# First and third LayerNorm of a decoder layer applied by ScalarE in two passes, and all step tables written anew

## The reference

```
x = layernorm(x + attention(x))       # 16 heads, causal, top-32 keys of each row kept
x = layernorm(x + experts(x, gate))   # 8 experts: relu(x W1_e) W2_e, times gate
x = layernorm(x + ffn(x))             # Hadamard turn, 4-bit rows, ternary weights

def _layernorm(x, axis=-1, eps=1e-05):
    m = jnp.mean(x, axis=axis, keepdims=True)
    v = jnp.var(x, axis=axis, keepdims=True)
    return (x - m) / jnp.sqrt(v + eps)
```

## Time and profile before

| what | value |
|---|---|
| runs of the kernel | 601.8, 604.54 and 602.76 us, median 602.76 |
| profiled execution | 602.27 us, its span from first to last instruction 600.5 us |
| PE busy | 528.7 us (88% of the span) |
| DVE busy | 460.9 us (77%) |
| ACT busy | 388.8 us (65%) |
| POOL busy | 344.8 us (57%) |
| mean granted clock of PE | 0.945 |
| DMA moved | 21.84 MB, mean 36 GB/s |

### The profile page before, as it was taken

The page is one execution under the profiler, slowest core; times in us unless marked ns, Lnnn a source line. Parts: engine busy times, 40 slices in busy tenths (PEclk is TensorE's granted clock), DMA queues, the critical chain, the costliest instruction groups (busy, mean ns, idle before and its releaser), DMA issues. The chain is left out here.

```text
span 600.5 us, 22290 instructions
## 1 busy us (share of the span) xinstructions
PE 528.7 (88%) x8180; PEld 451.2 (75%) x8180; DVE 460.9 (77%) x2867; ACT 388.8 (65%) x941; POOL 344.8 (57%) x336
## 2 busy tenths in 40 slices
PE   5577459999999989999999989998999999989941
PEld 3455337888778878887888878887888888878830
DVE  1777986868988997698889888989899998623213
ACT  2788765866667667675677657776686777555620
POOL 3458661975566646556375646665656556656831
PEclk9699757999999999999999999999999999999975
DMA  8253440010000010000100100010001000000000
GB/s 234 69 196 116 133 132 18 24 38 20 3 20 20 3 55 21 2 3 3 55 20 3 56 3 21 3 55 3 19 3 39 2 4 2 20 1 2 19 0 17
DMA packets 21932, 21.84 MB, mean 36 GB/s; under 512 B 1856, under 2 KB 19776, under 8 KB 21824
## 3 DMA queue, kind: packets, MB, share of 16 engines
q1 hardware_dynamic: 21824, 20.42, 10.9%
HBM read 18.32 MB, written 2.10 MB: 34 GB/s over the span
## 5 line engine op out<-in xcount | busy, mean ns | idle before, releaser
L484 POOL TENSOR_TENSOR h_lo<-h_raw,h_hi 128x512 f16<-128x512 f32 x128 | 149.1, 1167 | 126.5 <-ACT h_raw L607 125.4
L801 PE MATMUL ps_o<-w_hi,h_lo 128*128 128x256 f16 x512 | 139.8, 273 | 4.7 <-POOL h_lo L484 4.5
L785 PE MATMUL ps_z<-x1t_hi,w_lo 128*128 128x256 f16 x512 | 140.4, 274 | 0.7 <-DVE x1t_lo L951 0.7
L785 PE MATMUL ps_z<-x1t_lo,w_hi 128*128 128x256 f16 x512 | 140.1, 274 | 0.0
L785 PE MATMUL ps_z<-x1t_hi,w_hi 128*128 128x256 f16 x512 | 140.1, 274 | 0.0
L801 PE MATMUL ps_o<-w_lo,h_hi 128*128 128x256 f16 x512 | 139.6, 273 | 0.0
L801 PE MATMUL ps_o<-w_hi,h_hi 128*128 128x256 f16 x512 | 139.6, 273 | 0.0
L603 ACT ACTIVATE h_hi<-ps_z 128x512 f16<-128x512 f32 x128 | 76.0, 594 | 69.1 <-PE ps_z L785 69.1
L893 DVE MATCH_REPLACE8 taken<-next,taken 128x64 f32<-128x64 f32 (+4 forms) x480 | 110.5, 242 | 0.1
L505 POOL TENSOR_TENSOR acc<-go_sb,acc 128x512 f32<-128x512 f32 x56 | 71.4, 1274 | 58.2 <-ACT go_sb L617 57.4
L888 DVE MAX8 next<-taken 128x8 f32<-128x64 f32 (+4 forms) x480 | 85.3, 243 | 0.0
(11 more groups left out here) (118 smaller groups left out, 980.0 us busy)
## 6 DMA issues: line engine op xcount, KB each, us to landing
w_raw<-in_w1t SPq DMA_DIRECT2D x8, 512.0 KB, 4.3
w_raw<-in_w2t SPq DMA_DIRECT2D x8, 512.0 KB, 5.8
xt_sb<-in_xt SPq DMA_DIRECT2D x8, 256.0 KB, 3.4
x_sb<-in_x SPq DMA_DIRECT2D x8, 256.0 KB, 3.0
out<-out_sb SPq DMA_DIRECT2D x8, 256.0 KB, 2.2
xa_sb<-in_xt SPq DMA_DIRECT2D x7, 256.0 KB, 2.8
ctx_sb<-in_ctx_w SPq DMA_DIRECT2D x8, 128.0 KB, 3.0
itok_sb<-in_itok SPq DMA_DIRECT2D x8, 128.0 KB, 3.4
```

What stands on the lines that cost most here:

```text
L484: nc.gpsimd.tensor_tensor(h_lo[:, e % 2, 2 * z:2 * z + 2, :], h_raw[:, z, :, :], h_hi[:, e % 2, 2 * z:2 * z + 2, :], ALU.subtract)\
L785: last = pe.matmul(ps_z[z][:, d * UT:(d + 1) * UT], w[:, e, c, at:at + P], x[:, c, :], start=n == 0, stop=n == len(terms) - 1)
L801: last = pe.matmul(ps_o[e % 2][:, b * D:(b + 1) * D], h[:, e % 2, c, b * SEQ:(b + 1) * SEQ], w[:, e, c, :], start=n == 0, stop=n == len(te ...
```

## The change

The apply of the first LayerNorm in all units, and that of the third in units 0 to 6, moves from DVE to ACT. DVE did both sequences with one instruction each, (x - mean) x rstd. ACT does x + (-mean) for both sequences, waits for itself, and then multiplies by rstd in place. POOL makes -mean, one more small instruction between adding epsilon and the power. The second LayerNorm, and the third of the last unit, stay on DVE.

```diff
-    ("pe", "out_proj"), ("dve", "ln1_stats"), ("pool", "rstd1"), ("dve", "ln1_apply"), ("pe", "turn_x1"),
+    ("pe", "out_proj"), ("dve", "ln1_stats"), ("pool", "rstd1"), ("act", "ln1_apply"), ("pe", "turn_x1"),
...
-    ("pool", "rstd3"), ("dve", "ln3_apply"), ("sp", "store"),
+    ("pool", "rstd3"), ("act", "ln3_apply"), ("sp", "store"),
...
-                put(base + at[name], engine, name, v)
+                put(base + at[name], "dve" if name == "ln3_apply" and v == UNITS - 1 else engine, name, v)
...
+                    if i != 1:
+                        nc.gpsimd.tensor_scalar(minus_mean[:, i, :], meanvar[:, i, :, 0], -1.0, None, ALU.mult)\
+                            .then_inc(eps_added[i], 1)
-                    pool.wait_ge(eps_added[i], v + 1)
+                    pool.wait_ge(eps_added[i], (2 if i != 1 else 1) * (v + 1))
...
+            def layernorm_apply(i, dst, src, v, ready):
+                act.wait_ge(rstd_ready[i], v + 1)
+                for b in range(UB):
+                    last = act.activation(dst[:, b, :], src[:, b, :], ACT.Identity, bias=minus_mean[:, i, b:b + 1])
+                last.then_inc(centred[i], 1)
+                act.wait_ge(centred[i], v + 1)
+                for b in range(UB):
+                    last = act.activation(dst[:, b, :], dst[:, b, :], ACT.Copy, scale=rstd[:, i, b:b + 1])
+                last.then_inc(ready, 1)
```

All tables are new. Two lines of `STEADY` stand for them:

```diff
-    "rstd1": 38.75, "ln1_apply": 42, "turn_x1": 41.75, "x1t_high": 42, "x1t_low": 43, "gate_scale": 46.5,
+    "rstd1": 40.25, "ln1_apply": 39.5, "turn_x1": 42, "x1t_high": 41, "x1t_low": 44, "gate_scale": 48.75,
```

More of the change, by code:

```diff
@@ L106 @@
 STEADY = {
[L107 to L111, removed]
@@ L112 @@
-    "rstd1": 38.75, "ln1_apply": 42, "turn_x1": 41.75, "x1t_high": 42, "x1t_low": 43, "gate_scale": 46.5,
-    "experts": 44, "relu": 0, "h_low": 0, "gate_out": 0.5, "gated_add": 0.5, "ln2_stats": 77, "rstd2": 77.5,
[3 rows of a table removed]
+    "shift0": 0.75, "shift1": 0.25, "shift2": 0.5, "shift3": -1.25, "scores": -6.75, "copy_scores": -7, "exp": 4.75,
+    "select": 3, "pace": 0.875, "keep": 7.25, "turn_probs": 9.5, "copy_probs": 8.5, "turn_probs2": 10.75,
+    "copy_probs2": 10.25, "attend": 13, "normalise": 13.75, "load_xt": -13.25, "q": -11.75, "copy_q": -12.5,
@@ L117 @@
+    "spread_q": -11.75, "k": 44.75, "copy_k": -20.25, "v": 94.5, "copy_v": 94.75, "load_x": -4.5, "load_ctx": 23,
+    "x_plus_bo": 25.5, "gate_sums": 29.5, "turn_o": 36.75, "copy_ot": 35.75, "out_proj": 38.75, "ln1_stats": 39.5,
+    "rstd1": 40.25, "ln1_apply": 39.5, "turn_x1": 42, "x1t_high": 41, "x1t_low": 44, "gate_scale": 48.75,
+    "experts": 44, "relu": -0.5, "h_low": 0.5, "gate_out": -0.5, "gated_add": 1.5, "ln2_stats": 78.75, "rstd2": 78.5,
[3 rows of a table added]
 }
 FIRST = STEADY | {
-    "shift0": 2.5, "shift1": 1.25, "shift2": 0.5, "shift3": -0.25, "scores": -3, "copy_scores": -1.75, "select": 3,
@@ L120 @@
[L120 to L124, removed]
@@ L125 @@
-    "hadamard": 80.75, "copy_ot": 35.25, "spread_q": -14.5, "q": -16.5, "ffn_residual": 89.75, "copy_q": -9.75,
-    "load_ctx": 29.25, "ln3_stats": 97, "ffn": 88, "ln1_apply": 41.75,
+    "k": -7.75, "v": -2.5, "copy_v": -0.25, "exp": 6.5, "h_low": -2, "gate_sums": 25.75, "x1t_low": 43,
+    "ln1_apply": 40.75, "copy_probs": 9.25, "copy_ot": 36.75, "copy_probs2": 11.5, "out_proj": 40.25,
+    "normalise": 13.25, "load_x": 11.25, "select": 2, "shift3": -0.5, "x1t_high": 41.25, "turn_o": 38.75,
@@ new lines @@
+    "turn_o": 37, "load_xt": -21.75, "copy_probs2": 10.75, "shift2": 0, "out_proj": 38.5, "scores": -5.25,
+    "x_plus_bo": 9.25, "to_q4": 81.75, "copy_scores": -5.25, "normalise": 14.75, "copy_q4t": 88, "ffn_scale": 91.5,
+    "x1t_low": 44.25, "pace": 1.25, "ln3_stats": 105.25, "ln1_stats": 39.75, "x2t_high": 78.5, "load_x": -6.25,
+    "quantise": 82.75, "x2t_low": 82, "ln3_apply": 109.25, "gate_out": -1, "store": 132.25, "keep": 7,
+    "copy_k": -16.25, "v": 93, "k": 44.25, "turn_q4": 89.5, "ln1_apply": 40, "rstd3": 105.75, "ffn": 92,
@@ L136 @@
+    "gate_sums": 29, "x1t_high": 40.75,
 }
 LAST = STEADY | {
-    "shift2": 0, "normalise": 11.75, "x_plus_bo": 20.25, "gate_sums": 31.5, "experts": 43.75, "copy_probs": 8.75,
-    "turn_probs2": 9, "shift1": 0.25, "copy_k": -11, "ffn": 94.75, "out_proj": 38.5, "attend": 13.5, "to_q4": 87.25,
-    "rstd2": 76.75, "copy_scores": -6, "ffn_residual": 78.5, "exp": 5, "ffn_scale": 88, "turn_o": 37.25,
-    "turn_x2": 77.5, "copy_q4t": 89.25, "ln3_stats": 99.25, "copy_v": 32, "rstd1": 39.25, "store": 116.25,
@@ L142 @@
-    "ln1_apply": 41, "ln2_apply": 76.75, "quantise": 85.25, "ln2_stats": 71.5, "v": 11.75, "load_xt": -11.75,
-    "gate_scale": 49.75, "x2t_high": 82.5, "spread_q": -13.5, "rstd3": 98.75, "keep": 7.75, "copy_q": -12.25,
-    "ln1_stats": 37.5, "hadamard": 81.5, "k": 25, "x2t_low": 81.25, "gate_out": -0.5,
+    "shift1": 2.5, "exp": 2, "shift0": 3, "shift2": 1.5, "shift3": 1, "copy_q": -10.25, "turn_probs": 6.5,
+    "select": 0.5, "copy_probs": 5.25, "q": -8.75, "spread_q": -9, "copy_scores": -7.75, "scores": -8,
@@ L365, in decoder_layer @@
         rstd_ready = [sem(f"rstd_ready{i}") for i in range(3)]
+        centred = [sem(f"centred{i}") for i in range(3)]
         MISC = {
```

37 lines of the change are left out of this document (25 added, 12 removed), and 9 rows, old and new, of tables (SECOND, STEADY).

## The result

The changed kernel took 586.77 us in the median of 4 runs (585.7 to 590.07), the kernel before 602.85: a ratio of 0.973, with a 95% interval of 0.970 to 0.976. A second set of 6 runs (e1) gave 588.84 against 603.1, 0.976 (0.973 to 0.979). Medians and ratios are those of fast executions, and one slow execution of e16, of 2968 us, is left out.

A forecast was written before the change was run, and what follows sets the result against it. PE was taken as the bound from first expert matmul to last L2 (busy 464.17 of 477.5 us), after a chained head. Middle 6.4 plus head 4.1 gave 10.5: 602.3 - 10.5 = 591.8, range 588 to 595.5 (0.56).

The forecast's parts named there:

- (1): Sign on ACT: each apply runs as two pairs near 0.85 us each, with 0.03 between them.
- (2): Sign on PE: waits for x before turning x1 gone in units 1 to 7; about 0.3 us for h_lo instead.
- (3): Sign on PE: busy within 7 us of the length from the first L1 to the last L2.
- (4): Sign in the head: first L1 near 92 us, second mask on DVE near 39.6.
- (5): Sign at the end: the last unit's serial tail takes 27 to 28 us.
- The middle: First expert matmul to last L2: PE's waits at x1 turns shrink, 1.5 to 0.3 us in units 2 to 5; 6.4 gained.
- Rival D: More gain than forecast: the middle gives 10 of its 13.3 us and the head 6, 586.3; chance 0.10.
- The head: Chain through all engines before the first expert matmul: the new order gains 4.1 us, bounds -2 and 6.
- The walk's own 4.7: Head's new order laid along old durations to L1 of expert 3: 4.7 us gained, before allowing for low-clock steps.
- Third LayerNorm: hidden: Third apply on ACT, between an exp block and expert 1's relu: relu hidden with 1.8 us to spare.
- Rival C: Slower: ACT comes late to the apply behind an exp block; 0.7 us to spare in each unit; chance 0.08.
- The ScalarE rule: Skill's advice of VectorE for add and mul; without cover, seven hand-overs 1 us later each, 599.3.

The follow-up runs named there:

- e1: The changed kernel run again with no edit, for a second profile and more times: 588.84 us, ratio 0.976 to the kernel before.
- e16: The changed code with every engine's steps in the order of before, first and third applies on ScalarE: 617.12 us, ratio 1.023.
- e7: The changed kernel plus two unread tensor_scalar steps with constants on VectorE behind the first LayerNorm's sums: 587.13 us.
- e8: The changed kernel with VectorE waiting, without work, for GpSimd's 1/sigma behind the first LayerNorm's sums: 592.14 us.
- e11: The changed kernel plus four unread activations on ScalarE ahead of the first LayerNorm's apply: 595.02 us, ratio 0.986.
- e9: The changed kernel with the first apply back on VectorE, two steps later in its line in units 1 to 6: 590.89 us, ratio 0.981.
- e6: The changed kernel with only the third apply back on VectorE, in the same place of the order: 596.96 us, ratio 0.989.
- e3: The changed kernel's new order with both the first and third applies back on VectorE: 618.94 us, ratio 1.025 to the kernel before.
- e10: The changed kernel with both applies back on VectorE, each at a later place in its line: 594.37 us, ratio 0.984.
- e2: The changed kernel with only the first apply back on VectorE, ahead of the next unit's mask: 610.69 us, ratio 1.012.
- e18: The changed kernel with single-activation ScalarE applies and unread matmuls in the head's gaps on PE: 585.36 us, ratio 0.968.

## Why the prediction was right in direction and short in size

The mechanism was right; two terms of the sum were mis-sized. In units 2 to 5 x1 is turned after scores and half an L2, without waiting. The list of what would show it: (1) two pairs of 0.90, 0.04 between: right, 0.1 long in all. (2) The waits for x1 are gone in units 1 to 7; the wait for h_lo ahead of L2 of expert 7 is 0.14 and not 0.3. (3) PE is idle in 6.0 us of the stretch from the first L1: within 7. (4) The first L1 at 94.19 in the first profile, 93.54 in e1; 92 was forecast, and seen in e7 (92.4), e8 (92.8) and e11 (92.0). The second mask came at 42.03, 2.4 us later than worked out. (5) The tail is 27.7.

*The middle: 6.4 forecast, 9.4 measured.* This is the step that failed. Its "1.5 us wait becomes 0.3" counted idle time alone: 4 x 1.2 + 1.7 + 0.4 - 0.5. The idle time fell by 7.9. In units 2 to 5 it fell by 5.5 and not 4.8, for the wait left there is 0.14; the prediction's own numbers, h_lo at 284.95 and PE there at 284.86, gave 0.1. Units 1, 6 and 7 came out as worked out, and 0.8 lies in gaps that the sum didn't have. On top, PE's busy time for the same instructions fell by 1.5, a term that the sum put at nothing. A step that starts after a wait doesn't overlap the end of the one ahead: these matmuls take 0.27 us and start 0.11 apart, so 0.16 a wait, and nine waits over 0.15 us fewer make 1.4, an estimate that no run tests by itself. Rival D had 10 for the middle.

*The head: 4.1 forecast, 3.1 in the profiled run, 5.0 at the middle of seven profiles against the one of before.* The walk's own 4.7 was nearer than the 4.1 that I took from it. PE's waits for w_hi, which the walk was to shorten, went from 17.2 to 6.1 us (8.3 in e1). Its charge for slow steps was right in kind, but it could not be known from one profile. k of unit 0 took 1.99 us in the profile of before and 3.78 in the first of after: 1.8 of the 2.4 us by which the second mask was late. In e9 and e11, where it took 1.99, out_proj began at 79.7, as worked out; in the first profile at 81.3. That is luck, on the side of before. Which of the head's moves gave what is argued from the walk and not tested.

The profiles differ by 3.1 + 9.4 - 0.3 = 12.2 us. The medians differ by 14.3 to 16.1, since the profiled execution of after was the slowest of its four. So it came out close to rival D (586.3), held at 0.10, and just below a low end of 587.0 that D should have pulled down.

*"Third LayerNorm: hidden".* True for ScalarE, and the sum was not touched. But the text held the 15 to 20 us that leave VectorE for worth nothing, since it "was not the bound". e6 shows 9 us for the third apply alone, put on VectorE where ScalarE had it: the slack that counts is that of the step behind it, 0.9 to 1.0 us at both places, and not the stretch's average.

*Rival C's margin*, 0.7 us, is 0.9 in the profile (the prediction has x1 ready at 285.45 in one place and 285.6 in the other, and the first gives 0.85); e11, with about 1.3 more on the apply in the place where it stands, brought 0.3 us waits and no collapse.

*The ScalarE rule* (the Trainium skill, "ScalarE: Activation LUTs", Rules for kernel authors: VectorE for add and mul) would have put the applies on VectorE. The measurement decides against it for these places: 590.9 with the first apply on VectorE and 594.4 with both, 588 with ScalarE. That VectorE is quicker alone (0.4 us an instruction against 0.5) agrees; it didn't matter. The 599.3 that the prediction gives for seven hand-overs 1 us later each should be 598.8 (591.8 + 7).

## What to carry to other kernels

When work moves between two engines with lines of their own, ask of each line what stands next behind the moved step and how late that may be. Here that was 1.0 us, whatever the busy share said, and 3.3 us of lateness in each unit cost 22. Order and engine have to be judged together, and each half in a place made for it: the new order was 2.5% slower with VectorE in ScalarE's places (e3) and 1.6% faster with the same work a few steps later (e10). When adding up waits that go, take PE's length between two equal steps, and not its idle time; and when a forecast hangs on a head with idle gaps, take the profile's own head as one draw from a spread of several us.

## What the runs showed of the hardware

- In the kernel before, none of four idle gaps of 1.5 us in PE's middle was followed by a lower clock (1.00 over the middle). Of five gaps of 2.3 to 2.5 us in e2 three were (0.60 to 0.67 over the next 3.7 to 5.0 us), and of five gaps of 1.6 to 1.7 us in e16 one (0.55 over 3.8 us). So gaps of one length in one place of different units went either way.
- Matmuls that nobody reads, in the head's gaps, took about 3 us off the kernel, and did not put an end to slow steps (e18).
- A pair of tensor_scalar with columns took 0.73 us on VectorE alone. Where GpSimd's h_lo started 0.1 us behind it, the pair took 1.57, and 1.87 beside two h_lo in a row (e6). Where h_lo started 0.4 us behind it (e10, unit 1), the pair kept its 0.73 and h_lo took 1.33 in place of 1.16. A pair with constants took 0.46 (e7).
- ScalarE applies scale and bias by columns in one activation in 0.59 us, 0.09 more than with either alone.
